# Row stage of a graph network's first hypergraph convolution: grouped moments, a later projection, four banks

## The chip, the cores and the metric

The kernel runs on one core of one Trainium2 chip. Its metric is the device time of one execution in microseconds (us): the median of several runs. Before the change it is 4742.29 us (median of 3 runs, 4738.69 to 4744.97).

Names used below: TensorE (PE in the profile; PEld is its weight load), VectorE (DVE), ScalarE (ACT), GpSimd (POOL) and SyncE (SP), which here issues transfers only. SBUF is the on-chip memory of 128 partitions, PSUM the eight banks that TensorE writes to.

## The reference

A graph of 3125 nodes with 256 features and 50,000 edges goes through four residual layers. Each begins with a layer norm (without weights) and a relu. The fourth layer, cut to what matters here:

```python
h = jnp.maximum(_layernorm(x, axis=-1), 0.0)
x = x + _L3_gnn_ref(h, edge_index, edge_weight, ...)

def _hconv(x, src, dst, ew, w1, b1, w2, b2, g, b):
    h = jax.nn.relu(x @ w1 + b1)                     # rows: the stage of this change (first call)
    msg = ew[:, None] * h[src]
    agg = jax.ops.segment_sum(msg, dst, num_segments=x.shape[0])
    h = agg @ w2 + b2
    return jax.nn.relu(_bn(h, g, b))                 # batch norm over all nodes

h = _hconv(x, ..., c1_w1, c1_b1, ...)
h = jax.nn.relu(_bn(h, bn1_g, bn1_b))
h = _hconv(h, ..., c2_w1, c2_b1, ...)
h = _bn(h, bn2_g, bn2_b)
return jax.nn.relu(h + residual)
```

All of it is float32. The layer norm takes, for each node, mean and variance over its 256 features.

## The kernel before

The 3125 nodes are padded to 25 tiles (`NT`) of 128 rows; `X` holds all of them in SBUF, one tile being 128 partitions by 256 columns. The program is a sequence of phases. The last is `tail()` (from line 1461). In it each engine has its own list of instructions in one block (lines 1664 to 1768), and semaphores order the engines against each other; within an engine the written order holds. There is no planner: the order is written out by hand.

`tail()` does this, one after the other:

1. An aggregation (`add_steps`, `multiply_steps`, `gather_pairs`, `ready_pairs`, signals `agr`) that ends the third layer and adds into `X`. GpSimd gathers rows by indirect DMA, VectorE builds one-hot matrices (line 212), TensorE multiplies into the four PSUM banks `ps` (line 301), VectorE adds (line 228).
2. **The stage of this change**: layer norm and relu of `X`, and `relu(h @ w1 + b1)`, whose rows go to `feat_d` in device memory. The functions are `dve_normalise` (line 1527), `act_normalise` (1544) and `pe_normalise` (1562), called at lines 1728, 1704 and 1752.
3. The first convolution's aggregation, the same four functions, which gathers from `feat_d`; GpSimd starts when all five `stored` semaphores have counted every store (lines 1696 to 1698).
4. Its transposes and matmuls with `w2` (`pe_convolve`, `act_convolve`), two batch norms, and the second convolution's projection (`pe_project(pe, 1, n, ...)`, line 1760, with `dve_bias` at 1736 and `act_rectify` at 1716 and 1719).
5. Aggregation, matmuls and batch norms of the second convolution, and the output.

In stage 2 a tile goes through these steps: VectorE takes its moments (`bn_stats`, 1530) and puts them together (`bn_aggr`, 1538); ScalarE takes the square root (1548); VectorE takes the reciprocal (1535) and the shift, minus mean times reciprocal (1540); ScalarE normalises and rectifies into `HB` (1552); TensorE turns it by two transposes into a bank `pt` (1568); ScalarE copies that to `ht` (1558); TensorE projects it with two float32 matmuls, four instructions in the profile, into a bank `pf` (1524); VectorE adds the bias into one of five `stage` buffers (1519); ScalarE rectifies it in place (1514); SyncE stores it (1510).

The loops interleave tiles. In step j VectorE issues moments of tile j, bias of tile j - 3, reciprocal of tile j - 1, aggregate of tile j and shift of tile j - 1, with two `drain`s, which hold the engine until its earlier results are written. ScalarE issues root j, normalise j - 1, copy j - 2, rectify j - 4. TensorE turns tile n and then projects tile n - 1. `pt`, `pf` and `ht` have two buffers each. A bias waits for the projection of its tile and for the store that last used its `stage` buffer, five tiles earlier.

Of the kernel before, what the change touches and what calls it, by code (L numbers as in the profile page):

```python
# [5 lines left out]
ALU = mybir.AluOpType  # L6
# [7 lines left out]
P = 128  # L14
N = 3125
E = 50000
D = 256
HEADS = 4
HD = D // HEADS
KD = D // P  # L20
# [40 lines left out]
def gnn_program(nc, t, out):  # L61
# [1399 lines left out]
    def tail():  # L1461
# [16 lines left out]
        ht = sb("t_ht", [P, 2, D])  # L1478
# [7 lines left out]
        pf = [psum(f"t_pf{k}", [P, 512]) for k in range(2)]  # L1486
        feat_rows = feat_d.rearrange("(n p) f -> n p f", p=P)
# [28 lines left out]
        def dve_bias(dve, z, n):  # L1516
            dve.wait_ge(s_proj, NT * z + n + 1)
            wait_from(dve, stored[n % 5], 16 * (5 * z + n // 5))
            dve.tensor_tensor(stage[:, n % 5, :], pf[n % 2][:, 0:D], b1[:, z, :], ALU.add).then_inc(s_bias, 1)

        def pe_project(pe, z, n, source):
            wait_from(pe, s_bias, NT * z + n - 1)
            for c in range(KD):
                last = pe.matmul(pf[n % 2][:, 0:D], source(c), W1[:, z, c, :], start=(c == 0), stop=(c == KD - 1))
            last.then_inc(s_proj, 1)

        def dve_normalise(dve):
            for j in range(NT + 3):
                if j < NT:
                    dve.bn_stats(stats[:, j, :], X[:, j, :])  # L1530
                if j >= 3:
                    dve_bias(dve, 0, j - 3)
                if 1 <= j <= NT:
                    dve.wait_ge(s_root, j)
                    dve.reciprocal(rstd[:, j - 1:j], rstd[:, j - 1:j])
                dve.drain()
                if j < NT:
                    dve.bn_aggr(mv[:, j, :], stats[:, j, :]).then_inc(s_var, 1)
                if 1 <= j <= NT:
                    dve.scalar_tensor_tensor(out=shift[:, j - 1:j], in0=mv[:, j - 1, 0:1], scalar=-1.0,  # L1540
                                             in1=rstd[:, j - 1:j], op0=ALU.mult, op1=ALU.mult).then_inc(s_shift, 1)
                dve.drain()

        def act_normalise(act):
            for j in range(NT + 4):
                if j < NT:
                    act.wait_ge(s_var, j + 1)
                    act.activation(rstd[:, j:j + 1], mv[:, j, 1:2], ACT.Sqrt, bias=eps[:, 0:1]).then_inc(s_root, 1)
                if 1 <= j <= NT:
                    n = j - 1  # L1550
                    act.wait_ge(s_shift, n + 1)
                    act.activation(HB[:, n, :], X[:, n, :], ACT.Relu, bias=shift[:, n:n + 1],
                                   scale=rstd[:, n:n + 1]).then_inc(s_norm, 1)
                if 2 <= j <= NT + 1:
                    n = j - 2
                    act.wait_ge(s_ht, n + 1)
                    wait_from(act, s_proj, n - 1)
                    act.copy(ht[:, n % 2, :], pt[n % 2][:, 0:D]).then_inc(s_htc, 1)
                if j >= 4:
                    act_rectify(act, 0, j - 4)  # L1560

        def pe_normalise(pe):
            for n in range(NT + 1):
                if n < NT:
                    pe.wait_ge(s_norm, n + 1)
                    wait_from(pe, s_htc, n - 1)
                    for c in range(KD):
                        last = pe.transpose(pt[n % 2][:, c * P:(c + 1) * P], HB[:, n, c * P:(c + 1) * P], ident[:, :])
                    last.then_inc(s_ht, 1)
                if n >= 1:  # L1570
                    pe.wait_ge(s_htc, n)
                    pe_project(pe, 0, n - 1, lambda c: ht[:, (n - 1) % 2, c * P:(c + 1) * P])
# [236 lines left out]
```

## Time and profile before

| what | value |
|---|---|
| median of 3 runs | 4742.29 us |
| the profiled execution's own time | 4777.76 us |
| its span | 4775.9 us |
| busy share of the span: PE, PEld, DVE, ACT, POOL | 50%, 36%, 44%, 30%, 50% |
| mean granted clock of TensorE (1 is 2.4 GHz) | 0.706 |
| HBM traffic | 97 GB/s over the span |

The span runs from the first to the last instruction of one profiled execution; busy is time in which an engine worked on an instruction. The shares are means over phases that differ much, so a single stage has to be read from its own stretch. The granted clock is what the chip's throttle gave TensorE, as a share of full speed: 0.50 is 1.2 GHz. Times in rows are microseconds from the span's start.

### The profile page before, as it was taken

How to read it: one execution, taken by the hardware profiler on the slowest of the kernel's cores; microseconds unless marked ns; L12 is line 12 of the kernel's file. 1: busy time of each engine (PE TensorE's matmuls, PEld its weight loads, DVE VectorE, ACT ScalarE, POOL GpSimd, SP SyncE). 2: the span in 40 equal slices, each digit the busy share in tenths (PEclk: the TensorE clock that was granted, in tenths of full speed). 3: DMA queues.
4: the chain of work that ended last, by engine and by line, in shares of the span. 5: the costliest groups of instructions: out<-in, count | busy, mean ns of one | idle time of the engine just before them, and what ended most of it. 6: DMA issues, size and time to landing. Idle time of an engine off the chain costs nothing. (4 is left out here: it accounts for less than half of the span.)

```text
span 4775.9 us, 63970 instructions
## 1 busy us (share of the span) xinstructions
PE 2383.8 (50%) x11271; PEld 1719.6 (36%) x11272; DVE 2090.5 (44%) x5486; ACT 1423.7 (30%) x4674; POOL 2384.7 (50%) x2446
## 2 busy tenths in 40 slices
PE   4301546665431255555665825556535557445556
PEld 2201534444320154444443313334324334223334
DVE  6502974444330189444447613334213334223336
ACT  2201746666530155566666600000200000200002
POOL 4774015555547500455553466663166663466660
PEclk9655977777665588677767957667556678667667
DMA  3443433333234344233324833331133331223331
GB/s 113 123 107 93 128 107 93 101 101 97 65 89 118 108 116 127 83 98 98 102 80 115 273 92 91 90 91 57 53 91 90 90 91 43 92 85 90 91 90 38
DMA packets 339579, 465.59 MB, mean 97 GB/s; under 512 B 108191, under 2 KB 253928, under 8 KB 336112
## 3 DMA queue, kind: packets, MB, share of 16 engines
q0 software_dynamic: 113824, 289.70, 21.1%
q1 hardware_dynamic: 157536, 109.12, 8.1%
q10 hardware_dynamic: 67956, 64.45, 4.7%
q14 instruction: 243, 1.99, 0.1%
q8 instruction: 20, 0.33, 0.0%
HBM read 385.88 MB, written 76.97 MB: 97 GB/s over the span
## 5 line engine op out<-in xcount | busy, mean ns | idle before, releaser
L301 PE MATMUL t_ps<-t_ring,t_hot 128*128 x2640 | 891.1, 503 | 905.0 <-DVE t_hot L212 467.8
L153 POOL DMA_INDIRECT ring<-feat_d,srcC x784 | 754.6, 962 | 1084.0 <-ACTq L167 842.5
L301 PEld LDWEIGHTS t_ps<-t_ring,t_hot 128*128 128x128 f32 x2640 | 644.7, 255 | 1152.2 <-issue 1036.4
L153 POOL DMA_INDIRECT t_ring<-feat_d,srcC x784 | 741.9, 946 | 563.7 <-issue 218.3
L175 ACT ACTIVATE ring<-ring,exC 128x64 f32<-128x64 f32 x3136 | 818.9, 338 | 113.4 <-issue 110.5
L301 PE MATMUL bank<-ring,arena 128*128 x1760 | 648.8, 505 | 109.6 <-ACT ring L175 52.8
L910 PE MATMUL wide<-arena 128*128 128x100 bf16 x4704 | 272.9, 216 | 462.5 <-issue 228.4
L509 POOL DMA_INDIRECT attr_d<-abuf,attr_pos x392 | 405.6, 1035 | 191.6 <-issue 129.2
L228 DVE TENSOR_TENSOR acc<-acc,t_ps 128x256 f32 x440 | 184.4, 419 | 715.0 <-DMA arena<-in_L_gnn_ar 212.4
L153 POOL DMA_INDIRECT t_ring<-rel_d,relC x392 | 371.2, 947 | 227.4 <-issue 115.1
L301 PEld LDWEIGHTS bank<-ring,arena 128*128 128x128 f32 x1760 | 406.1, 256 | 188.8 <-issue 133.7
L212 DVE TENSOR_SCALAR t_hot<-lane,dlocT,weightT 128x128 f32<-128x128 f32 x1320 | 409.1, 356 | 103.0 <-issue 71.1
L291 PE MATMUL wide<-arena 128*128 x880 | 244.1, 369 | 414.7 <-DVE arena L220 311.9
L910 PEld LDWEIGHTS wide<-arena 128*128 128x128 bf16 x4704 | 237.2, 102 | 498.6 <-issue 285.2
L291 PEld LDWEIGHTS wide<-arena 128*128 128x128 f32 x880 | 209.7, 257 | 521.7 <-issue 486.7
L1602 ACT COPY t_ring<-t_pt 128x256 f32<-128x256 f32 x26 | 9.6, 370 | 1204.0 <-PE t_pt L1593 1204.0
L877 DVE TENSOR_TENSOR arena<-wide,masks 128x800 f32<-128x800 f32 x196 | 191.0, 974 | 308.0 <-remote 306.7
L228 DVE TENSOR_TENSOR acc<-acc,bank 128x261 f32 x440 | 187.6, 426 | 229.3 <-issue 117.8
L228 DVE TENSOR_TENSOR X<-X,t_ps 128x256 f32 x220 | 92.0, 418 | 359.7 <-DMA X<-in_x 206.4
L206 DVE TENSOR_TENSOR arena<-lane,dlocT 128x256 f32<-128x256 f32 x440 | 185.2, 421 | 117.5 <-issue 103.1
L829 ACT ACTIVATE arena<-arena,ones 128x512 bf16<-128x512 bf16 x196 | 141.9, 724 | 289.6 <-remote 282.7
L220 DVE TENSOR_SCALAR arena<-lane,arena,minus_tile 128x128 f32<-128x128 f32 x440 | 159.1, 361 | 137.9 <-issue 81.2
(266 smaller groups left out, 2271.0 us busy)
## 6 DMA issues: line engine op xcount, KB each, us to landing
arena<-lo_d ACTq DMA_DIRECT2D x392, 128.0 KB
rel_d<-mid_stage SPq DMA_DIRECT2D x25, 1024.0 KB, 4.4
arena<-attr_d SPq DMA_DIRECT2D x98, 260.0 KB
abuf<-in_attr SPq DMA_DIRECT2D x56, 448.0 KB
ring<-feat_d,srcC POOLq DMA_INDIRECT x784
t_ring<-feat_d,srcC POOLq DMA_INDIRECT x784
feat_d<-arena ACTq DMA_DIRECT2D x50, 128.0 KB
feat_d<-t_stage SPq DMA_DIRECT2D x50, 128.0 KB, 1.7
```

Source lines behind the costliest of these rows:

```text
L153: pool.indirect_dma_start(out=ring[:, u % RING, j, 0:D], out_offset=None, in_=table, in_offset=bass.IndirectOffsetOnAxis(ap=index[:, u, j: ...
L175: last = act.activation(part_of_row, part_of_row, ACT.Copy, scale=exC[:, bass.ds(u, 1), j, h])
L206: last = dve.tensor_tensor(hot[:, k % NHOT, :, :], lane[:, :].unsqueeze(1).to_broadcast([P, 2, P]), dlocT[:, bass.ds(s, 1), :].rearrange(" ...
L212: last = dve.tensor_scalar(hot[:, k % NHOT, j, :], lane[:, :], dlocT[:, bass.ds(s, 1), j], weightT[:, bass.ds(s, 1), j], ALU.is_equal, ALU ...
L220: dve.tensor_scalar(hot_a[:, k % NHOT, :], lane[:, :], aring[:, slot, AW - 1:AW], minus_tile[:, g.attr, bass.ds(s, 1)], ALU.subtract, ALU. ...
L228: dve.tensor_tensor(acc[:, tile, 0:g.width], acc[:, tile, 0:g.width], ps[k % NHOT][:, 0:g.width], ALU.add).then_inc(g.added, 1)
L291: pe.matmul(ps_a[k % NHOT][:, 0:AW - 1], hot_a[:, k % NHOT, :], aring[:, slot, 0:AW - 1], start=True, stop=True).then_inc(g.attr_done, 1)
L301: last = pe.matmul(ps[k % NHOT][:, 0:g.width], hot[:, k % NHOT, j, :], ring[:, slot, j, 0:g.width], start=(j == 0), stop=(j == 1))
L509: pool.indirect_dma_start(out=attr_d, in_=abuf[:, g % 2, k, :], in_offset=None, out_offset=bass.IndirectOffsetOnAxis(ap=attr_pos[:, at + k ...
L829: act.activation(looked[:, k % 2, 1, :], apart[:, k % 2, :], ACT.Relu, scale=-1.0, bias=ones[:, 0:1]).then_inc(s_dst_hot[l], 1)
L877: dve.tensor_tensor(cand[:, k % 2, :, :, :], pk[k % 2][:, :, :].rearrange("p b (s x) -> p (b s) x", x=P)[:, :, 0:HEADS * NT] .rearrange("p ...
L910: last = pe.matmul(pk[k % 2][:, j // 2, at:at + HEADS * NT], looked[:, k % 2, q, j * P:(j + 1) * P], tab[:, piece, q * HEADS * NT:(q + 1) ...
```

## The change

Buffers: `ht` grows from two tiles to four. The turn uses four banks, `pt` and the aggregation's `ps[2:4]`; the projection uses four, `pf` and `ps[0:2]`. The waits for a bank or a buffer now look back four tiles and not two, in the second convolution's projection too.

VectorE: the 25 tiles are divided in four groups (0 to 1, 2 to 7, 8 to 15, 16 to 24). For each group it takes all moments, drains once, puts all of them together, signals once, waits for one square root over the whole group, and takes one reciprocal and one shift over the group. In the last group the biases of tiles 0 to 4 stand behind the moments of tiles 20 to 24; the other twenty biases follow behind the group.

ScalarE: one square root per group, in front of the steps j = 0, 1, 4 and 9. Step j then has normalise j, copy j - 1, rectify j - 5.

TensorE: turn n, then projection n - 2.

```diff
@@ -1475,7 +1475,7 @@
         b2 = sb("t_b2", [P, 2, KD])
         gb = sb("t_gb", [P, 2, 2, 2, KD])
         eps = sb("t_eps", [P, 2])
-        ht = sb("t_ht", [P, 2, D])
+        ht = sb("t_ht", [P, 4, D])
         stage = sb("t_stage", [P, 5, D])
         tmp = sb("t_tmp", [P, 3, D])
         bn = sb("t_bn", [P, KD, NR, 6])
@@ -1484,6 +1484,8 @@
         ps = [psum(f"t_ps{k}", [P, 512]) for k in range(NHOT)]
         pt = [psum(f"t_pt{k}", [P, 512]) for k in range(2)]
         pf = [psum(f"t_pf{k}", [P, 512]) for k in range(2)]
+        p_turn, p_proj = pt + ps[2:4], pf + ps[0:2]
+        LN_GROUPS = [(0, 2), (2, 8), (8, 16), (16, NT)]
         feat_rows = feat_d.rearrange("(n p) f -> n p f", p=P)
 
         g_rel = Steps("agr", life, False)
@@ -1516,60 +1518,71 @@
         def dve_bias(dve, z, n):
             dve.wait_ge(s_proj, NT * z + n + 1)
             wait_from(dve, stored[n % 5], 16 * (5 * z + n // 5))
-            dve.tensor_tensor(stage[:, n % 5, :], pf[n % 2][:, 0:D], b1[:, z, :], ALU.add).then_inc(s_bias, 1)
+            dve.tensor_tensor(stage[:, n % 5, :], p_proj[n % 4][:, 0:D], b1[:, z, :], ALU.add).then_inc(s_bias, 1)
 
         def pe_project(pe, z, n, source):
-            wait_from(pe, s_bias, NT * z + n - 1)
+            wait_from(pe, s_bias, NT * z + n - 3)
             for c in range(KD):
-                last = pe.matmul(pf[n % 2][:, 0:D], source(c), W1[:, z, c, :], start=(c == 0), stop=(c == KD - 1))
+                last = pe.matmul(p_proj[n % 4][:, 0:D], source(c), W1[:, z, c, :], start=(c == 0), stop=(c == KD - 1))
             last.then_inc(s_proj, 1)
 
+        def group_of(n):
+            return next(g for g, (a, b) in enumerate(LN_GROUPS) if a <= n < b)
+
         def dve_normalise(dve):
-            for j in range(NT + 3):
+            def roots(g):
+                a, b = LN_GROUPS[g]
+                dve.wait_ge(s_root, g + 1)
+                dve.reciprocal(rstd[:, a:b], rstd[:, a:b])
+                dve.drain()
+                dve.scalar_tensor_tensor(out=shift[:, a:b], in0=mv[:, a:b, 0], scalar=-1.0, in1=rstd[:, a:b],
+                                         op0=ALU.mult, op1=ALU.mult).then_inc(s_shift, 1)
+
+            biased = 0
+            for g, (a, b) in enumerate(LN_GROUPS):
+                for n in range(a, b):
+                    dve.bn_stats(stats[:, n, :], X[:, n, :])
+                    if g == len(LN_GROUPS) - 1 and n >= a + 4:
+                        dve_bias(dve, 0, biased)
+                        biased += 1
+                dve.drain()
+                for n in range(a, b):
+                    last = dve.bn_aggr(mv[:, n, :], stats[:, n, :])
+                last.then_inc(s_var, 1)
+                roots(g)
+            for n in range(biased, NT):
+                dve_bias(dve, 0, n)
+
+        def act_normalise(act):
+            for j in range(NT + 5):
+                for g, (a, b) in enumerate(LN_GROUPS):
+                    if j == (0, 1, 4, 9)[g]:
+                        act.wait_ge(s_var, g + 1)
+                        act.activation(rstd[:, a:b], mv[:, a:b, 1], ACT.Sqrt, bias=eps[:, 0:1]).then_inc(s_root, 1)
                 if j < NT:
-                    dve.bn_stats(stats[:, j, :], X[:, j, :])
-                if j >= 3:
-                    dve_bias(dve, 0, j - 3)
-                if 1 <= j <= NT:
-                    dve.wait_ge(s_root, j)
-                    dve.reciprocal(rstd[:, j - 1:j], rstd[:, j - 1:j])
-                dve.drain()
-                if j < NT:
-                    dve.bn_aggr(mv[:, j, :], stats[:, j, :]).then_inc(s_var, 1)
-                if 1 <= j <= NT:
-                    dve.scalar_tensor_tensor(out=shift[:, j - 1:j], in0=mv[:, j - 1, 0:1], scalar=-1.0,
-                                             in1=rstd[:, j - 1:j], op0=ALU.mult, op1=ALU.mult).then_inc(s_shift, 1)
-                dve.drain()
-
-        def act_normalise(act):
-            for j in range(NT + 4):
-                if j < NT:
-                    act.wait_ge(s_var, j + 1)
-                    act.activation(rstd[:, j:j + 1], mv[:, j, 1:2], ACT.Sqrt, bias=eps[:, 0:1]).then_inc(s_root, 1)
+                    act.wait_ge(s_shift, group_of(j) + 1)
+                    act.activation(HB[:, j, :], X[:, j, :], ACT.Relu, bias=shift[:, j:j + 1],
+                                   scale=rstd[:, j:j + 1]).then_inc(s_norm, 1)
                 if 1 <= j <= NT:
                     n = j - 1
-                    act.wait_ge(s_shift, n + 1)
-                    act.activation(HB[:, n, :], X[:, n, :], ACT.Relu, bias=shift[:, n:n + 1],
-                                   scale=rstd[:, n:n + 1]).then_inc(s_norm, 1)
-                if 2 <= j <= NT + 1:
-                    n = j - 2
                     act.wait_ge(s_ht, n + 1)
-                    wait_from(act, s_proj, n - 1)
-                    act.copy(ht[:, n % 2, :], pt[n % 2][:, 0:D]).then_inc(s_htc, 1)
-                if j >= 4:
-                    act_rectify(act, 0, j - 4)
+                    wait_from(act, s_proj, n - 3)
+                    act.copy(ht[:, n % 4, :], p_turn[n % 4][:, 0:D]).then_inc(s_htc, 1)
+                if j >= 5:
+                    act_rectify(act, 0, j - 5)
 
         def pe_normalise(pe):
-            for n in range(NT + 1):
+            for n in range(NT + 2):
                 if n < NT:
                     pe.wait_ge(s_norm, n + 1)
-                    wait_from(pe, s_htc, n - 1)
+                    wait_from(pe, s_htc, n - 3)
                     for c in range(KD):
-                        last = pe.transpose(pt[n % 2][:, c * P:(c + 1) * P], HB[:, n, c * P:(c + 1) * P], ident[:, :])
+                        last = pe.transpose(p_turn[n % 4][:, c * P:(c + 1) * P], HB[:, n, c * P:(c + 1) * P],
+                                            ident[:, :])
                     last.then_inc(s_ht, 1)
-                if n >= 1:
-                    pe.wait_ge(s_htc, n)
-                    pe_project(pe, 0, n - 1, lambda c: ht[:, (n - 1) % 2, c * P:(c + 1) * P])
+                if n >= 2:
+                    pe.wait_ge(s_htc, n - 1)
+                    pe_project(pe, 0, n - 2, lambda c: ht[:, (n - 2) % 4, c * P:(c + 1) * P])
 
         def pe_convolve(pe, z):
             def chunk(r):
```

## Rows read from the trace of the kernel before

**Rows 1.** Timeline at the start of the stage: start us, us, engine, line, operation.

```profile
3326.75 0.43 DVE L1530 BATCH_NORM_STATS2 stats<-X 128x6 f32<-128x256 f32 x1
3327.25 0.18 DVE L1538 BATCH_NORM_AGGREGATE mv<-stats 128x2 f32<-128x6 f32 x1
3327.52 1.28 ACT L1548 ACT_TABLE_LOAD   x1 [600.76 <-DVE mv L1538]
```

**Rows 2.** Timeline at the end of the stage and the first gather behind it.

```profile
3424.90 3.62 PE L1524 MATMUL t_pf<-t_w,t_ht 128*128 128x256 f32 x8
...
3429.02 0.42 ACT L1514 ACTIVATE t_stage<-t_stage 128x256 f32<-128x256 f32 x1 [1.29 <-DVE t_stage L1519]
...
3431.90 0.97 POOL L153 DMA_INDIRECT t_ring<-feat_d,srcC  x1 [132.90 <-DMA feat_d<-t_stage]
```

**Rows 3.** Windows: length, busy of PE, PEld, DVE, ACT, POOL, granted clock, DMA.

```profile
3334.00:3380.00 46.00, 26.39 (x67) 16.50 (x67) 13.42 (x60) 15.58 (x46) 0.00 (x0) 0.50 0.08 29
```

**Rows 4.** Waits around the stage: who waits for whom, total us, times, longest.

```profile
DVE t_stage L1519 <- PE t_pf L1524: 68.1, 25, 3.3
```

**Rows 5.** Timeline, one period in the stage's middle, and the next period's first operation.

```profile
3358.04 0.42 DVE L1519 TENSOR_TENSOR t_stage<-t_pf,t_b 128x256 f32<-128x256 f32 x1 [2.75 <-PE t_pf L1524]
3358.38 0.15 DVE L1535 RECIPROCAL rstd<-rstd 128x1 f32<-128x1 f32 x1
3358.61 0.18 DVE L1538 BATCH_NORM_AGGREGATE mv<-stats 128x2 f32<-128x6 f32 x1
3358.70 0.13 DVE L1540 SCALAR_TENSOR_TENSOR shift<-mv,rstd 128x1 f32<-128x1 f32 x1
3358.82 0.30 ACT L1548 ACTIVATE rstd<-mv,t_eps 128x1 f32<-128x1 f32 x1 [2.69 <-DVE mv L1538]
...
3359.03 0.59 ACT L1552 ACTIVATE HB<-X,shift,rstd 128x256 f32<-128x256 f32 x1
3359.52 0.35 ACT L1558 COPY t_ht<-t_pt 128x256 f32<-128x256 f32 x1
...
3359.67 0.69 PE L1568 MATMUL t_pt<-ident,HB 128*128 128x128 f32 x2 [1.66 <-ACT HB L1552]
3359.77 0.42 ACT L1514 ACTIVATE t_stage<-t_stage 128x256 f32<-128x256 f32 x1
...
3362.10 0.42 DVE L1519 TENSOR_TENSOR t_stage<-t_pf,t_b 128x256 f32<-128x256 f32 x1 [2.75 <-PE t_pf L1524]
```

**Rows 6.** The projection's banks: one projection matmul, duration ns min/median/max.

```profile
L1524 PE MATMUL t_pf<-t_w,t_ht x100: 631/634/656, 3331.7 to 3427.9; 128*128 128x256 f32 x100
```

**Rows 7.** Line 1568, the turn's transposes, duration ns min/median/max.

```profile
L1568 PE MATMUL t_pt<-ident,HB x50: 273/421/477, 3330.5 to 3424.7; 128*128 128x128 f32 x50
```

**Rows 8.** Timeline, start of the second convolution's projection.

```profile
4077.34 14.83 PE L1524 MATMUL t_pf<-t_w,t_ring 128*128 128x256 f32 x56 [15.63 <-ACT t_ring L1624]
...
4081.16 0.42 DVE L1519 TENSOR_TENSOR t_stage<-t_pf,t_b 128x256 f32<-128x256 f32 x1 [1.28 <-PE t_pf L1524]
...
4082.71 0.42 DVE L1519 TENSOR_TENSOR t_stage<-t_pf,t_b 128x256 f32<-128x256 f32 x1 [1.13 <-PE t_pf L1524]
...
4083.58 0.42 DVE L1519 TENSOR_TENSOR t_stage<-t_pf,t_b 128x256 f32<-128x256 f32 x1 [0.44 <-PE t_pf L1524]
```

**Rows 9.** Timeline, first turns behind each convolution's aggregation.

```profile
4026.77 0.66 PE L1593 MATMUL t_pt<-ident,acc 128*128 128x128 f32 x4 [0.65 <-DVE acc L228]
4027.25 0.37 ACT L1602 COPY t_ring<-t_pt 128x256 f32<-128x256 f32 x1 [597.82 <-PE t_pt L1593]
...
4701.39 0.37 ACT L1602 COPY t_ring<-t_pt 128x256 f32<-128x256 f32 x1 [598.81 <-PE t_pt L1593]
```

**Rows 10.** Windows: the first convolution's matmuls and the second projection.

```profile
4020.00:4077.00 57.00, 36.33 (x135) 20.17 (x133) 30.17 (x72) 24.40 (x45) 5.44 (x1) 0.90 0.00 1
4077.00:4103.00 26.00, 24.33 (x100) 20.24 (x100) 10.61 (x25) 17.70 (x38) 0.00 (x0) 0.90 0.35 121
```

**Rows 11.** Line 1510, the stores of finished rows: issue to landing.

```profile
DMA to landing us min/median/max: 1.7/1.7/1.8
```

## The prediction

> **What bounds the kernel now.** I first looked at which stretch the change touches, then at who waits for whom in it, then at one period of its loop. The stretch is the one in which the first convolution's rows are made: from the first moments (`bn_stats`, 3326.75) to the last rectification (3429.02 + 0.42 = 3429.44), 102.7 us [rows 1, 2]. I count t from 3326.75, so it ends at t = 102.7. In its middle no engine is full: of 46 us TensorE is busy 26.4, VectorE 13.4, ScalarE 15.6, at a granted clock of 0.50, which is 1.2 GHz [rows 3]. VectorE alone waits 68.1 us in 25 waits for the projection [rows 4]. One period shows why [rows 5]: bias (3358.04), reciprocal, aggregate (3358.61), square root (3358.82, after 2.69 us of waiting for that aggregate), normalise (3359.03), copy (3359.52), and the next bias at 3362.10, after 2.75 us of waiting for the projection that follows the copy. That is 4.06 us, all of it a ring through three engines: VectorE puts the next tile's aggregate behind the bias, the bias waits for the projection, and the projection waits for a copy that ScalarE issues behind a square root that needs that aggregate. 25 tiles cost 25 x 4.06 = 101.5 us: the ring is the stage.
>
> When the stage ends, GpSimd's first gather starts 2.46 us later, at 3431.90 [rows 2]. It waits for the last store, so every microsecond taken from the stage moves all that follows.
>
> **The change, part by part.**
>
> *The ring is cut.* No bias stands ahead of a moment that an earlier tile still needs, except five in the last group. What is left per tile are three independent rates. ScalarE: normalise to copy 0.49, copy to rectify 0.25, rectify 0.42 [rows 5] less the same overlap of 0.10, so 0.32: 1.06 us. Twenty-one of 25 square roots go (0.30 us each, off the path by then). VectorE: one operation of 256 columns per 0.34 us (bias 3358.04, reciprocal 3358.38 [rows 5]); bias and moments together 0.68, later the bias alone. TensorE at 1.2 GHz: eight projection matmuls take 3.62 us with 0.634 for one [rows 2, 6], so (3.62 - 0.63) / 7 = 0.427 each, 1.71 us a tile; its two turns take 0.69 us [rows 5] with 0.42 to 0.48 for one [rows 7], 0.21 to 0.27 apart, taken as 0.25 each: together 2.21 us. At 2.4 GHz: the same four matmuls, in the second convolution's projection, come every 0.87 us (biases at 4082.71 and 4083.58) [rows 8], and turns stand 0.13 apart ((0.66 - 0.27) / 3) [rows 7, 9]; with 0.27 for two, 1.14 us a tile. So TensorE is the next bound at either clock, just ahead of ScalarE at the upper one.
>
> *Which clock.* In the second projection TensorE comes out of 15.6 us without work, and its biases at 4081.16 and 4082.71 stand 1.55 us apart; from 4082.71 they stand 0.87 apart. So some 5.4 us of unbroken matmuls (4077.34 to 4082.7) stood before the full rate, and it held to the end at 0.90 mean [rows 8, 10]. In the convolution, with TensorE busy 36.3 of 57 us, the clock is 0.90 too [rows 10]. After the change TensorE has a queue of work from t = 7, and at the low clock it needs more time than it gets tiles, so it doesn't pause until the clock has risen. I take the rise at t = 12.3.
>
> *The head, step by step* (starts in t; hand-over between engines 0.03 to 0.11, estimated from [rows 1, 5]). Group of tiles 0 and 1: moments 0.00 and 0.34, aggregates 0.84 and 0.94 (0.50 from the last moment to the first aggregate [rows 1], 0.10 from one small operation to the next [rows 5]), table load of 1.28 at 1.21, root 2.49, reciprocal 2.82, shift 3.06, normalise 0 at 3.22. Group of 6: from 3.16, 6 x 0.34 + 0.16 + 6 x 0.10, last aggregate ends 6.04; ScalarE is held in front of tile 1 for it; root 6.07, normalise 1 at 6.27, turn 1 at 6.97. Group of 8: VectorE takes 6.74 to 10.5; root 10.53; shift 11.10. Group of 9: five moments to 12.9, then four moments and five biases in turn. The biases need projections 0 to 4. TensorE: turns 1, 2, projection 0 (1.71), turn 3, projection 1 to about 12.0 at the low clock, then 1.14 a tile, so projection 4 ends near 16.0. Bias 4 at 16.2, drain, nine aggregates to 17.6; root; normalise 9 at 17.9. ScalarE's rectifications 0 to 3, which stand ahead of that root in its queue, are done by 17.0. TensorE has by then eight turns and seven projections behind it: 8 x 0.27 + 7 x 0.87 = 8.2 us at the upper clock, and 2.6 more for 5.3 us at the lower, out of 11.6: it hardly idles.
>
> *The rest.* Turn 9 at 18.6; then 16 x 0.27 = 4.3 for turns and 18 projections x 0.865 = 15.6 bring TensorE to 38.5. The last matmul's length over its spacing 0.2 (0.634 less 0.427), bias 0.42, rectify 0.42, hand-overs 0.06: the stage ends at t = 39.6 in place of 102.7. That is 63.1 us less. The last store and the first gather keep their 2.46 us.
>
> *What I cost at nothing.* Four banks in place of two: the two added pairs are the aggregation's, which has ended before and has not begun after; VectorE's last bias stands ahead of the first add in its queue. Stores: a tile's 128 KB land in 1.7 us [rows 11], a stage buffer is wanted again five tiles, so 5 x 1.14 = 5.7 us, later; between a turn's end and its bias five tiles on lie 4.3 us, against about 2.6 for copy, rectification, issue and landing. If that cover went (landing above 3.4 us) each tile would pay a fifth of the excess. The second convolution's projection keeps its matmul rate: VectorE waits for TensorE at its biases [rows 8], so two more banks bring 0. The clock handed to the aggregation behind: it costs nothing, because ScalarE's idle time over the first convolution's aggregation, entered at a low clock, is 597.8 us and over the second's, entered at 0.90, 598.8 [rows 9].
>
> *A rule weighed.* The rows show turns 0.13 us apart, 0.66 us for four, right behind an aggregation [rows 9]. The Trainium skill (TensorE: Matmul & The Clock Gate, Part 4: PE-mode transpose) says that the full clock doesn't engage for transposes. The trace disagrees with it where turns are mixed with matmuls; by the rule the turns would stay 0.25 apart, and the sum would be 50 x 0.12 = 6 us less gain.
>
> **Bounds of the sum.** Best: the clock is high throughout and the head costs TensorE nothing, 7.0 + 24 x 0.27 + 25 x 0.87 + 1.1 = 36.3, a gain of 66. Worst for the clock is the first rival.
>
> **Rivals.**
> 1. *The clock stays at 1.2 GHz.* The head's pauses, or the turns among the matmuls, keep it low, as in this stage before [rows 3]. TensorE from t = 7.0: 24 x 0.50 + 25 x 1.71 = 54.8, plus 1.1: end at 62.9, gain 39.8, 4702.5 us. For it: it is what this stage showed. Against: TensorE would then be at work without a break, and [rows 8] shows the rise in that case.
> 2. *A shorter ring binds.* If ScalarE's copy of a tile has to come before the normalise of the next, each tile costs turn 0.27, copy 0.25 + 0.1, rectify 0.32, normalise 0.59, hand-over 0.11: 1.65 us. I count it as going round once per two tiles, as ScalarE's order has normalise one tile ahead of copy; if once per tile, 16 x (1.65 - 1.14) = 8 us are lost: 4687 us.
> 3. *Slower: the stores.* Bias n waits for store n - 5, and rectification now stands a step later. The stage would be longer than before if five tiles took over 20.3 us, so if a store landed later than about 18 us after issue. At a spacing of 0.87 us they land in 1.7 [rows 8, 11]; at 19 us each the stage would be 25 x 4.3 = 108 us, 4747 us. Only a transfer slowed tenfold does it.
> 4. *It doesn't do what it says:* another wait keeps the 4.06 us period, 4742 us. The order of the instructions leaves no ring that closes within one tile, and the 4.06 us rest on one.
>
> **How the numbers follow.** The profiled execution took 4777.76 us with a span of 4775.9; the median of the runs is 4742.29, 0.7% below. The stage holds no gathers, and I subtract its gain whole from the median: 4742.3 - 63.1 = 4679.2 (the profiled one would be 4714.7). Small hand-overs are more often left out than counted twice, so I say 4680. Chances: the forecast (4674 to 4685) 0.70; rival 2, or a head some microseconds longer (to 4692), 0.13; rival 1, or a clock that changes back and forth (4690 to 4706), 0.13; rival 3 0.02; rival 4 0.02. The range takes in rival 1's price: 4674 to 4703. What a measurement of this kernel can tell from no change is about 0.2%, 9.5 us; all of the first three cases lie beyond it: faster 0.96, same 0.02, slower 0.02.
>
> **What would show it.** The stretch from the first moments to the last rectification is about 40 us long. The four square roots stand near t = 2.5, 6.1, 10.5 and 17.6, and normalise 9 just behind the last. Between t = 20 and 38 biases are 1.14 us apart, TensorE is busy without a gap at a clock near 1, projection matmuls last 0.38 and not 0.63 us. VectorE's wait for projections is below 20 us. Biases 2.2 us apart with matmuls of 0.63 are rival 1; biases 1.6 apart with gaps on TensorE in front of turns rival 2; VectorE waiting for stores rival 3. The aggregation behind should keep its 598 us; if it is 5 us or more off, the prediction misses a coupling.

## The result

The changed kernel takes 4673.6 us (median of 4 runs, 4656.7 to 4681.82), the kernel before, in its runs of then and now, 4743.63 us: ratio 0.9852, 95% interval 0.9829 to 0.9875. By the medians that is 70.0 us less, where 63 were forecast; the interval reaches from 4662.5 to 4684.3 us (0.9829 and 0.9875 of 4743.63). The profiled execution took 4672.72 us (span 4671.0).

The first group is the timeline of the stage's head in the changed kernel (start us, us, engine, line, operation). It answers to [rows 1].

```profile
3298.32 0.75 DVE L1544 BATCH_NORM_STATS2 stats<-X 128x6 f32<-128x256 f32 x2
3299.15 0.25 DVE L1550 BATCH_NORM_AGGREGATE mv<-stats 128x2 f32<-128x6 f32 x2
3299.48 1.28 ACT L1561 ACT_TABLE_LOAD   x1 [594.63 <-DVE mv L1550]
3300.78 0.29 ACT L1561 ACTIVATE rstd<-mv,t_eps 128x2 f32<-128x2 f32 x1
...
3301.54 0.60 ACT L1564 ACTIVATE HB<-X,shift,rstd 128x256 f32<-128x256 f32 x1 [0.47 <-DVE shift L1538]
...
3303.55 0.51 DVE L1550 BATCH_NORM_AGGREGATE mv<-stats 128x2 f32<-128x6 f32 x6
3304.09 0.30 ACT L1561 ACTIVATE rstd<-mv,t_eps 128x6 f32<-128x6 f32 x1 [1.95 <-DVE mv L1550]
...
3304.94 0.69 PE L1580 MATMUL t_pt<-ident,HB 128*128 128x128 f32 x2 [2.24 <-ACT HB L1564]
...
3308.23 0.30 ACT L1561 ACTIVATE rstd<-mv,t_eps 128x8 f32<-128x8 f32 x1 [1.44 <-DVE mv L1550]
...
3314.57 0.30 ACT L1561 ACTIVATE rstd<-mv,t_eps 128x9 f32<-128x9 f32 x1
3314.78 0.58 ACT L1564 ACTIVATE HB<-X,shift,rstd 128x256 f32<-128x256 f32 x1
```

The second is the timeline of one period in the middle, then the last rectification and the first gather; it answers to [rows 2, 5].

```profile
3323.27 0.61 ACT L1564 ACTIVATE HB<-X,shift,rstd 128x256 f32<-128x256 f32 x1
3323.28 1.03 PE L1526 MATMUL t_ps<-t_w,t_ht 128*128 128x256 f32 x4
3323.76 0.37 ACT L1570 COPY t_ht<-t_pt 128x256 f32<-128x256 f32 x1
...
3324.01 0.44 ACT L1516 ACTIVATE t_stage<-t_stage 128x256 f32<-128x256 f32 x1
3324.14 0.38 PE L1580 MATMUL t_pt<-ident,HB 128*128 128x128 f32 x2
...
3324.34 0.42 DVE L1521 TENSOR_TENSOR t_stage<-t_ps,t_b 128x256 f32<-128x256 f32 x1 [0.66 <-PE t_ps L1526]
3324.36 1.03 PE L1526 MATMUL t_ps<-t_w,t_ht 128*128 128x256 f32 x4
...
3335.54 0.42 ACT L1516 ACTIVATE t_stage<-t_stage 128x256 f32<-128x256 f32 x1 [0.79 <-DVE t_stage L1521]
...
3338.42 0.94 POOL L153 DMA_INDIRECT t_ring<-feat_d,srcC  x1 [67.60 <-DMA feat_d<-t_stage]
```

The stage runs from 3298.32 to 3335.54 + 0.42 = 3335.96, 37.64 us, against 102.7: 65.1 us less. The first gather follows 2.46 us behind it, as before. The ring is gone: a tile takes TensorE 1.08 us (3323.28 and 3324.36), and it goes from projection to turn to projection (3323.28, 3324.14, 3324.36). ScalarE's 1.06 us a tile (3323.27, 3323.76, 3324.01, and the next normalise at 3324.33, which isn't shown) is just below it. In the head one sees the four roots (t = 2.5, 5.8, 9.9 and 16.3 from 3298.32) and normalise 9 right behind the last, at t = 16.46.

The windows of the changed kernel (length, busy time and count of PE, PEld, DVE, ACT, POOL, granted clock, DMA share, GB/s; they answer to [rows 3]) show the clock's way through the stage:

```profile
3298.30:3304.30 6.00, 0.41 (x2) 0.20 (x2) 3.81 (x18) 2.39 (x5) 0.00 (x0) 0.87 0.00 0
3304.30:3309.80 5.50, 4.79 (x15) 3.60 (x16) 4.79 (x23) 4.03 (x11) 0.00 (x0) 0.52 0.00 0
3309.80:3315.40 5.60, 5.60 (x31) 4.32 (x29) 5.03 (x24) 4.76 (x14) 0.00 (x0) 1.00 0.22 75
3315.40:3334.00 18.60, 18.60 (x103) 15.94 (x103) 7.56 (x19) 17.91 (x51) 0.00 (x0) 1.00 0.35 120
```

The clock is 1.00 until 3302.7, so still at turn 0 (3302.29), then 0.50 until 3309.5, from turn 1 (3304.94) on, and 1.00 again from 3309.6 (t = 11.2). TensorE is busy without a gap for the last 18.6 us shown. VectorE's waits for projections, 68.1 us before [rows 4], are 11.1 us (total, times, longest):

```profile
DVE t_stage L1521 <- PE t_ps L1526: 5.8, 9, 0.7
DVE t_stage L1521 <- PE t_pf L1526: 5.3, 8, 0.7
```

### The profile page after: what moved, and what is told of

Its sections match the earlier page's. It is cut to its first block and busy times, and to the rows that moved or that the text cites. A ratio compares the mean times of both kernels' runs of the same rounds, so it can differ in the third digit from the quotient of the medians.

```text
span 4671.0 us, 63853 instructions
## 1 busy us (share of the span) xinstructions
PE 2342.8 (50%) x11271; PEld 1694.6 (36%) x11272; DVE 2088.9 (45%) x5444; ACT 1410.8 (30%) x4653; POOL 2384.8 (51%) x2446
## 5 line engine op out<-in xcount | busy, mean ns | idle before, releaser
L234 DVE TENSOR_TENSOR acc_a<-acc_a,wide 128x129 f32 x440 | 127.5, 290 | 200.2 <-issue 129.2
```

What stands on the lines that cost most here:

```text
L234: dve.tensor_tensor(acc_a[:, tile, :], acc_a[:, tile, :], ps_a[k % NHOT][:, 0:AW - 1], ALU.add).then_inc(g.attr_added, 1)
```

## The experiments

Each stage length is that of one profiled execution. Each experiment was read twice: by the length of the stage in its trace, from the first moments to the last rectification (two executions of the changed kernel further down gave 37.85 and 37.68 us, so this repeats to 0.2 us), and by the time of the whole kernel, where the runs of one kernel lie 6 to 25 us apart. All ratios are to the kernel before on the same chip.

| kernel | stage us | time us | before us | ratio, 95% interval |
|---|---|---|---|---|
| before | 102.7 | 4743.63 | | |
| changed | 37.64 | 4673.6 | 4743.63 | 0.9852, 0.9829 to 0.9875 |
| e1, groups alone | 40.01 | 4710.28 | 4771.91 | 0.9867, 0.9836 to 0.9898 |
| e2, depth alone | 99.94 | 4765.03 | 4771.91 | 0.998, 0.9966 to 0.9995 |
| e3, depth and a late bias | 39.86 | 4707.81 | 4771.91 | 0.9858, 0.9832 to 0.9883 |
| e4, the change again | 37.85 | 4704.31 | 4771.91 | 0.9851, 0.9829 to 0.9873 |
| e7, bias five behind | 43.04 | 4704.38, one run | 4774.29 | |
| e8, before, TensorE kept busy | 80.07 | 4750.75 | 4774.29 | 0.9945, 0.9926 to 0.9965 |
| e6, change, busy start | 37.29 | 4718.8, one run | 4774.29 | |
| e5, shorter head | 38.62 | 4714.93 | 4774.29 | 0.9873, 0.9853 to 0.9892 |
| e9, head mended | 37.22 | 3529.39, one run | 3598.05 | |
| e10, the same and a busy start | 38.38 | 3534.89 | 3598.05 | 0.9829, 0.9816 to 0.9843 |
| e11, the change, third time | 37.68 | 3534.2 | 3598.05 | 0.9819, 0.9805 to 0.9833 |
| e12, rectification later | 36.66 | 3532.5 | 3598.15 | 0.9821, 0.9808 to 0.9835 |

### Which part of the change does it: e1, e2, e3, e7

e1 keeps the groups and takes back the depth:

```diff
-        p_turn, p_proj = pt + ps[2:4], pf + ps[0:2]
+        p_turn, p_proj = pt, pf
...
-                if n >= 2:
-                    pe.wait_ge(s_htc, n - 1)
-                    pe_project(pe, 0, n - 2, ...)
+                if n >= 1:
+                    pe.wait_ge(s_htc, n)
+                    pe_project(pe, 0, n - 1, ...)
```

> Grouped moments, grouped roots and late biases as in the change; but two banks and two turn buffers, and the projection one tile behind the turn, as before. Theory (the gain is that no bias stands any more in front of a moment, aggregate or shift in VectorE's queue): the stage from the first moments to the last rectification takes 38 to 42 us, against 102.7 before and 37.6 with the change, since only the head waits more for its banks; the time is within 0.2% of the changed kernel's. Rival (depth: banks and the later projection carry the gain): the stage takes over 60 us.

40.01 us: of the 65.1 us the groups alone bring 62.7. TensorE then stands once 1.55 and once 0.83 us in front of a projection until a bias has freed its bank, together 2.4 us, as much as the depth brings on top. (Not among the lines above: `ht` and the waits for banks go back to two as well.)

e2 keeps the depth and takes back the groups; VectorE and ScalarE go tile by tile as before, one step later (these lines against the kernel before):

```diff
-            for j in range(NT + 3):
+            for j in range(NT + 4):
                 if j < NT:
                     dve.bn_stats(stats[:, j, :], X[:, j, :])
-                if j >= 3:
-                    dve_bias(dve, 0, j - 3)
+                if j >= 4:
+                    dve_bias(dve, 0, j - 4)
```

> Four banks, four turn buffers and the projection two tiles behind the turn, as in the change; but moments, roots and shifts tile by tile as before, with each bias again in front of the next reciprocal and shift (bias of tile j - 4 in step j, one later than before as the projection is one later). Theory (order on VectorE): the ring through three engines is still closed within one tile, 3.3 to 4.1 us a tile at the low clock, the stage 85 to 103 us and the time within 0.4% of the kernel before. Rival (depth carries the gain): under 60 us for the stage, about 4680 us or below.

99.94 us: depth alone brings 2.8 us. Its timeline has the old period (the next bias stands 4.06 us on, at 3365.61), the bias with its wait for TensorE again in front of aggregate and shift:

```profile
3361.55 0.42 DVE L1521 TENSOR_TENSOR t_stage<-t_ps,t_b 128x256 f32<-128x256 f32 x1 [2.74 <-PE t_ps L1526]
...
3362.12 0.18 DVE L1543 BATCH_NORM_AGGREGATE mv<-stats 128x2 f32<-128x6 f32 x1
...
3362.54 0.58 ACT L1557 ACTIVATE HB<-X,shift,rstd 128x256 f32<-128x256 f32 x1
...
3363.18 0.69 PE L1573 MATMUL t_ps<-ident,HB 128*128 128x128 f32 x2 [1.66 <-ACT HB L1557]
...
3363.66 1.91 PE L1526 MATMUL t_pf<-t_w,t_ht 128*128 128x256 f32 x4
```

It also corrects one member of the ring. The prediction lets the projection wait for ScalarE's copy. In e2 that copy was made a tile earlier, and yet the projection starts 0.48 us behind the turn (3363.18, 3363.66), as it does in the kernel before (3359.67 in [rows 5], and this row):

```profile
3360.15 1.92 PE L1524 MATMUL t_pf<-t_w,t_ht 128*128 128x256 f32 x4
```

So what closes the ring on TensorE is its own order: bias, aggregate, root, normalise, then the turn of that tile, and the projection that stands behind this turn. That is why projecting a tile later and having more banks brought next to nothing.

e3 differs from e2 in one number on VectorE: the bias of tile j - 6 stands in step j, not that of j - 4 (rectification follows, at j - 7).

> As the run with depth alone (four banks, projection two behind, moments tile by tile, nothing grouped), with one edit: the bias of tile j - 6 stands in step j instead of j - 4. Theory: grouping is not needed, what counts is that the ring closes over three tiles; the pace is then set by ScalarE's 1.27 us or VectorE's 1.25 us a tile, 1.3 to 1.5 us, so the stage takes 42 to 50 us and most of the gain is there (4678 to 4690 us). Rival (the grouped moments carry it by saving drains, roots and hand-overs): over 70 us for the stage.

39.86 us, 60.1 less than e2, with nothing grouped. The theory holds; the stage came out 2 us below its range, as the pace was 1.21 to 1.25 us a tile. (The whole kernel's 4707.81 us lies above the 4678 to 4690 expected, because the kernel before takes 4771.91 us on this chip; the gain is 64.1 us.) The timeline shows why: the same operations in the same order (bias, aggregate), but the bias has nothing to wait for. What holds the pace instead stands in the window below it: ScalarE is busy 10.00 of 10.00 us.

```profile
3340.63 0.41 DVE L1521 TENSOR_TENSOR t_stage<-t_pf,t_b 128x256 f32<-128x256 f32 x1
...
3341.18 0.18 DVE L1543 BATCH_NORM_AGGREGATE mv<-stats 128x2 f32<-128x6 f32 x1
...
3341.84 0.41 DVE L1521 TENSOR_TENSOR t_stage<-t_ps,t_b 128x256 f32<-128x256 f32 x1
```

```profile
3340.00:3350.00 10.00, 10.00 (x50) 6.80 (x50) 8.59 (x43) 10.00 (x34) 0.00 (x0) 1.00 0.29 102
```

e7 puts the bias at j - 5 (rectification at j - 6).

> As the run with the late bias, but bias of tile j - 5 in step j, so that the ring closes over two tiles and not one or three. Theory (pace is the ring's length over the tiles that it spans, until an engine is full): a ring of 4.1 us at the low clock gives 2.05 us a tile, under TensorE's own 2.2, so TensorE is full, its clock rises, the ring shortens to about 3 us and the pace falls to 1.25 to 1.5 us: a stage of 40 to 47 us. Rival (anything in front of the shift in VectorE's queue costs its whole wait): over 60 us.

43.04 us, inside the range, at 1.48 us a tile with the clock at 1.00 (25 us from 3325). The two biases shown are two tiles apart, 2.96 us, which is the ring; in each a bias waits 0.28 us for TensorE, and no engine is full (TensorE 21.75, ScalarE 22.60 of 25 us):

```profile
3335.47 0.42 DVE L1521 TENSOR_TENSOR t_stage<-t_pf,t_b 128x256 f32<-128x256 f32 x1 [0.28 <-PE t_pf L1526]
...
3338.43 0.42 DVE L1521 TENSOR_TENSOR t_stage<-t_ps,t_b 128x256 f32<-128x256 f32 x1 [0.28 <-PE t_ps L1526]
```

One tile more between a bias and what it waits for is worth 56.9 us (from e2), the second 3.2 us. In these three runs the pace is the ring's length over the tiles that it spans, until an engine is full, and grouping is one of two ways out of the ring. They don't end at the same bound: the change is held by TensorE at 1.08 us a tile, e3, with a root per tile, by ScalarE at 1.25. That the stages still lie only 2.2 us apart is because e3's head has no groups to wait for (argued, not tested). Of e3's time some 1.3 us is a wait for a store at the end (2.3 us long, the last projection being done 2.57 us before the end of the stage and not 1.25 as in the change).

### How much of it is the clock: e8, e6

```diff
                     pe_project(pe, 0, n - 1, ...)
+                    for k in range(2):
+                        pe.matmul(ps[0][:, 0:D], ident[:, :], W1[:, 0, 0, :], start=True, stop=True)
```

> The kernel before, with two more float32 matmuls of 256 columns behind each projection, whose product nobody reads (they stand in TensorE's idle 1.66 us of each period). It tells how much of the 65 us is the low clock alone. Theory (the clock is an effect of the ring and lengthens it): the granted clock rises to near 1, projection 1.92 to 1.03 us and turns 0.69 to 0.4, so the period falls from 4.06 to about 3.05 us and the stage from 102.7 to 75 to 82 us, 20 to 28 us faster than before, although TensorE does more. Rival (the clock doesn't rise, or the ring isn't TensorE's): the stage stays at 100 us or grows to 105.

The stage falls to 80.07 us, 22.7 us less, by giving TensorE more to do; ratio 0.9945 (0.9926 to 0.9965). Its timeline and window:

```profile
3365.96 1.03 PE L1574 MATMUL t_ps<-t_w,ident 128*128 128x256 f32 x4
3366.16 0.42 DVE L1519 TENSOR_TENSOR t_stage<-t_pf,t_b 128x256 f32<-128x256 f32 x1 [1.74 <-PE t_pf L1524]
...
3367.15 0.58 ACT L1552 ACTIVATE HB<-X,shift,rstd 128x256 f32<-128x256 f32 x1
...
3368.06 1.11 PE L1524 MATMUL t_pf<-t_w,t_ht 128*128 128x256 f32 x4
...
3369.21 0.42 DVE L1519 TENSOR_TENSOR t_stage<-t_pf,t_b 128x256 f32<-128x256 f32 x1 [1.73 <-PE t_pf L1524]
```

```profile
3335.00:3400.00 65.00, 49.05 (x214) 35.69 (x213) 24.41 (x106) 28.21 (x83) 0.00 (x0) 0.98 0.12 41
```

The period is 3.05 us, the projection takes 1.1 us and not 1.92, the granted clock is 0.98. The two added matmuls (3365.96 to 3366.99) are done before the tile behind them is normalised, so they hold nothing up. So of the 65.1 us that the change brings, 22.7 can be had by the clock alone with the ring left as it is, and 42.4 need the ring to be cut. The low clock was an effect of the ring and made it a third longer; the prediction took both together, through the rate at the upper clock.

e6 is the changed kernel with ten such matmuls before its first turn.

> The changed kernel with ten float32 matmuls of 256 columns, read by nobody, before TensorE's first turn, so that it comes into the head at the high clock. Theory (in the head VectorE and ScalarE set the pace, TensorE has slack): the stage takes 37.3 to 37.8 us, the same as with the change, and TensorE shows longer gaps before turns of tiles 1 to 9. Rival (the cold head costs what it takes more, 2.6 us): about 35 us.

37.29 us, at the lower edge of the range, 0.35 below the change. That is less of a test than it was meant to be: behind a pause of 2.30 us in front of turn 1 the clock fell again, from 3337.5 to 3340.8 (t = 10.0). So the low stretch was halved, 3.3 us in place of 6.8, and the stage became 0.35 us shorter; a head that is at the high clock throughout is seen only in e10, with another order.

### Is there more than the stage: e4, e11

> The changed kernel itself, to tell whether its 70 us of gain, against 65.05 us in the stage's own stretch, are real beyond the stage. Theory: the rest is scatter of the gather phases, which the change doesn't touch: over these runs the median gain comes to 60 to 70 us, the stage again takes 37.5 to 37.8 us, and the three aggregations of the last phase move by several us from one execution to the next in no relation to the change. Rival (the denser stage also speeds the aggregation behind it): the first convolution's aggregation is shorter than the second's by 3 us or more, and the gain is 68 to 75 us.

> The changed kernel itself, on the chip of the two runs above. The stage takes 37.6 to 37.9 us. Its gain over the kernel before is 63 to 70 us if the stage is all there is; over 70 us again would speak for an effect beyond it, in the aggregations behind.

By the medians the gains are 67.6 us (e4) and 63.9 us (e11). ScalarE stands idle through each aggregation behind the stage, so its idle time at the first copy gives the length. Two rows of the changed kernel's timeline, answering to [rows 9]:

```profile
3930.49 0.37 ACT L1615 COPY t_ring<-t_pt 128x256 f32<-128x256 f32 x1 [594.53 <-PE t_pt L1606]
...
4596.44 0.37 ACT L1615 COPY t_ring<-t_pt 128x256 f32<-128x256 f32 x1 [590.77 <-PE t_pt L1606]
```

The first convolution's took 597.8 us before and 594.5 here, the second's 598.8 and 590.8; and the aggregation in front of the stage, which the change can't touch, 600.8 [rows 1] and 594.6 (3299.48 in the head above). All three were shorter in this one execution (3.3, 8.0 and 6.2 us), the one in front no less than the others. The rival wants the first to be at least 3 us shorter than the second. In e4 it is 596.1 against 597.9, in e11 500.8 against 499.5, in the profiled execution of the change 3.8 us longer, and before the change it was 1.0 shorter. The gains of e4 and e11 are short of the rival's 68 us too. A second reading says the same: from the stage's end to the kernel's end the execution of the change took 1335.0 us, but e4 1343.3, e1 1343.7, e3 1344.1, e5 1345.1, e7 1345.6 and e6 1349.0 with a short stage, and e2 and e8, with a long one, 1343.8 and 1343.7. So the rival is refuted, and what lies between 65 and 70 us is scatter of phases that the change leaves alone. (These are executions of their own: the profiled one of the kernel before took 4777.76 us, more than any of the four runs in its median.)

### A version meant to be better: e5, e9, e10, e12

e5 loads ScalarE's square root table ahead of the phase, takes the second and the third root one step later and makes two more biases early.

```diff
+                act.wait_ge(s_eps, 1)
+                act.activation(bsc[:, 0, 0:1], eps[:, 0:1], ACT.Sqrt, bias=eps[:, 0:1])
                 ready_pairs(act, "agr", g_rel, ring)
...
-                    if j == (0, 1, 4, 9)[g]:
+                    if j == (0, 2, 5, 9)[g]:
...
-                    if g == len(LN_GROUPS) - 1 and n >= a + 4:
+                    if g == len(LN_GROUPS) - 1 and n >= a + 2:
```

> A version meant to be better: the changed kernel with ScalarE's square root table loaded at the start of the phase (one root of a constant, read by nobody), the second group's root behind normalise 1 and not in front of it (steps 0, 2, 5, 9), and seven early biases, two moments earlier. Theory (the head of 16 us is a chain of table load, moments and roots): the table load's 1.28 us goes and TensorE starts tile 1 about 2 us earlier; the stage takes 34.5 to 36.2 us, which the time of the whole kernel (scatter 20 us) can hardly show. Rival (TensorE's or ScalarE's total is what counts from the first tile): 36.3 us or more, only the table load's share.

38.62 us, 1 us worse than the change. The early biases run at TensorE's pace, and the last group's aggregates stand behind them; ScalarE waits 2.52 us for those and TensorE 2.14 for ScalarE. It is the old fault once more, inside the head: a bias that waits, in front of aggregates.

```profile
3345.82 0.42 DVE L1521 TENSOR_TENSOR t_stage<-t_pf,t_b 128x256 f32<-128x256 f32 x1 [0.33 <-PE t_pf L1526]
...
3346.91 0.42 DVE L1521 TENSOR_TENSOR t_stage<-t_ps,t_b 128x256 f32<-128x256 f32 x1 [0.33 <-PE t_ps L1526]
3347.43 0.71 DVE L1550 BATCH_NORM_AGGREGATE mv<-stats 128x2 f32<-128x6 f32 x9
3348.17 0.30 ACT L1561 ACTIVATE rstd<-mv,t_eps 128x9 f32<-128x9 f32 x1 [2.52 <-DVE mv L1550]
...
3349.01 0.44 PE L1580 MATMUL t_pt<-ident,HB 128*128 128x128 f32 x2 [2.14 <-ACT HB L1564]
```

e9 takes that away: three early biases (`n >= a + 6`) and roots at steps (0, 2, 5, 8).

> The shorter head again, with what held it taken away: seven early biases had put two that wait for projections in front of the last group's aggregates. Now the table load is ahead of the phase, the roots stand at steps 0, 2, 5 and 8, and only three biases (tiles 0 to 2) stand in front of the last aggregates. Theory (a waiting bias in front of the aggregates costs its wait, in the head as in the old ring): TensorE's 2.1 to 2.5 us gap before tile 9 goes and the stage takes 35.6 to 36.6 us, against 38.62 in the run with seven and 37.7 to 37.9 with the change. Rival (the fewer early biases hold TensorE for its banks): 37.5 us or more.

37.22 us, below the rival's 37.5 but not in the theory's 35.6 to 36.6. The gap before tile 9 is gone and one before tile 6 has come: bias 0 is now late, ScalarE's rectification 0 waits for it, and normalise 6 is queued behind the rectification.

```profile
2350.11 0.41 DVE L1521 TENSOR_TENSOR t_stage<-t_pf,t_b 128x256 f32<-128x256 f32 x1
...
2350.55 0.42 ACT L1516 ACTIVATE t_stage<-t_stage 128x256 f32<-128x256 f32 x1 [1.97 <-DVE t_stage L1521]
...
2350.87 0.58 ACT L1564 ACTIVATE HB<-X,shift,rstd 128x256 f32<-128x256 f32 x1
...
2351.51 0.44 PE L1580 MATMUL t_ps<-ident,HB 128*128 128x128 f32 x2 [1.39 <-ACT HB L1564]
```

e10 is e9 with the ten matmuls of e6.

> The mended head with ten matmuls of 256 columns, read by nobody, in front of TensorE's first turn. Alone they brought 0.4 to 0.5 us. Theory (with the shorter head TensorE is what everything waits for sooner, so its low clock costs more): the stage takes 34.4 to 35.8 us, 2 to 3 us less than the change. Over the whole kernel that is 0.06%, which its time won't show: the ratio to the kernel before should be that of the change within its interval. Rival: TensorE's pause between tiles 1 and 2 lets the clock fall again, and the stage takes what it takes without the added matmuls (35.6 us or more).

38.38 us, worse than e9: the theory fails. The rival's lower bound (35.6 us) is met, and the clock did fall, but not behind the pause that the rival names (between tiles 1 and 2, 1.54 us). The head runs at a clock of 1.00, so TensorE comes to the gap before tile 6 earlier and stands 2.24 us; after it the clock falls, and 3.2 us (2353.0 to 2356.2) run at the low rate. Its windows, and two rows of its timeline:

```profile
2345.00:2351.00 6.00, 4.77 (x24) 3.57 (x24) 5.48 (x25) 3.05 (x9) 0.00 (x0) 1.00 0.01 1
2351.00:2357.00 6.00, 4.76 (x17) 3.90 (x18) 3.74 (x19) 4.91 (x14) 0.00 (x0) 0.72 0.25 87
2357.00:2375.00 18.00, 18.00 (x100) 15.49 (x99) 7.02 (x17) 17.51 (x49) 0.00 (x0) 1.00 0.34 117
```

```profile
2352.24 0.44 PE L1580 MATMUL t_ps<-ident,HB 128*128 128x128 f32 x2 [2.24 <-ACT HB L1564]
...
2354.23 1.92 PE L1526 MATMUL t_pf<-t_w,t_ht 128*128 128x256 f32 x4
```

e12 is e9 with rectification one step later in ScalarE's queue (tile j - 6 in step j).

> The mended head with one more edit: rectification of tile j - 6 in ScalarE's step j instead of j - 5. In the mended head ScalarE waited 1.97 us in front of rectification 0 for bias 0, with normalise 6 queued behind it, and TensorE then stood 1.39 us in front of tile 6. Theory (the same rule as for the ring, a waiting operation costs what is queued behind it): normalise 6 no longer stands behind that wait, TensorE's gap before tile 6 shrinks to under 0.5 us, and the stage takes 35.3 to 36.3 us against 37.22. Rival (TensorE then waits for its banks instead, as projection 4 needs bias 0): 36.8 us or more. The time of the whole kernel stays within the interval of the changed one's.

36.66 us, the shortest stage of all, 1.0 us below the changed kernel in e11 (on another chip, where the kernel before takes the same time), 0.4 us above the range of the theory and below the rival's. TensorE has no gap from its third turn on (2347.94, t = 5.9) to its last projection. That is worth 0.6 of the 1.0 us; the other 0.4 stand at the very end, where the last bias waits 0.2 us for a store and not 0.85 as in e11. What is left of the head is the low clock, which lasted until t = 12.0. Over the whole kernel, 3532.5 us against 3534.2 tells nothing; the better version is shown in its stage alone.

## Why the prediction was wrong where it was

- **The step that failed: "I subtract its gain whole from the median".** That puts at nothing, without a reason, what a median of whole runs carries from the phases outside the stage. With the stage as measured it would have given 4742.3 - 65.1 = 4677.2, inside the range; 4.9 of the 70.0 us that the medians show lie outside the stage. The runs show scatter there: the changed kernel's four lie 25.1 us apart, those of before 6.3 (15.8 with the fourth), and the same code in front of the stage took from 3324.2 to 3339.7 us in the four runs of one chip (e1 to e4). The lower end, 4674, lies 2.3 us below the prediction's own best case (4742.3 - 66 = 4676.3), while the prediction puts at 9.5 us what a measurement can tell apart. The median came out 0.4 us below that end; forecast and sum (4680 and 4679.2) lie within the measured interval, 4662.5 to 4684.3. On which side of 4674 the median fell was luck. What sets the time of the untouched phases from run to run stays open.
- **The sum, a smaller step: 63.1 forecast, 65.1 measured in the stage.** It stayed within the best case, 66. The mis-sized term is the head: 17.9 us forecast for normalise 9, 16.46 measured. Of these 1.4 us, 1.2 stand already at bias 4 (16.2 forecast, 14.99 measured), which waits for projection 4. From projection 1's end, about 12.0, three tiles of 1.14 us give 15.4 and not the 16.0 written down; and TensorE was at that point by 11.6, as the clock had risen at t = 11.2 and not 12.3. The rest is the small operations: an aggregate takes (0.51 - 0.15) / 5 = 0.07 us and not 0.10. Behind the head TensorE took 1.08 us a tile and not 1.14, which the store at the end (below) in part takes back. "Small hand-overs are more often left out than counted twice" led to 4680 from 4679.2, and was the wrong way.
- **The ring and its cut: right, but for one member.** The bias in front of the next aggregate closes it: e2 has the ring with all the depth, e3 is free of it with nothing grouped. The projection was held by the turn in front of it, not by the copy (e2).
- **TensorE as the next bound, clock near 1: right.** 1.08 us a tile against 1.14 forecast; ScalarE 1.06 as worked out.
- **Rival 1 (low clock):** did not come; e8 gives its measure, 22.7 us of the old stage. **Rival 2 (a shorter ring):** there is none in the steady part. In the head waits of this kind exist, as e5 and e9 show. **Rival 3 (stores):** nearer than the prediction thought, which costed them at nothing. A store lands in 1.7 us as a rule, but in up to 3.1 in the changed kernel and 3.5 in e3 (1.8 at most before [rows 11]). In the change one bias (24) waits 0.78 us for a store, of which 0.34 delay the end; in e3 it is 2.3 us. **Rival 4:** no.
- **The Trainium skill's rule on transposes** (TensorE: Matmul & The Clock Gate, Part 4: PE-mode transpose): the turns lie 0.11 us apart at a granted clock of 1.00 ((1.08 - 0.87) / 2), so the trace stays against it for turns mixed with matmuls. A long stretch of turns alone is in no run here.

## What to carry to other kernels

In a loop over several engines whose instructions run in the written order, find the operation that waits for the slowest hand-over and look at what is queued behind it that an earlier stage of the next tile needs: moving that one operation back by one or two tiles can be worth more than all banks and buffers. Look also at which instruction the slow hand-over really waits behind: an engine's own order can hold it where the program's wait doesn't. Don't read the granted clock as a given: here the ring left TensorE idle for part of each period, the clock stood at 0.50 and made the ring a third longer, and work that nobody reads raised it to 0.98. When the range of a forecast is worked out from one stage, add the scatter of the medians: here the interval was 22 us wide, and the stage was missed by 2.

## What the runs showed of the hardware

- On the two chips of e9 to e12 the kernel before takes 3598.05 and 3598.15 us and not 4771.91, with the same program. The aggregations of this phase take some 500 us there and not 597 (ScalarE's idle time over the last one: 499.5 in e11, 597.9 in e4); the stage takes 37.68 us as elsewhere, and the change's gain in microseconds is nearly the same (63.9 and 67.6), so its ratio differs. Why the gathers are faster there was not examined.
- The clock can fall behind a pause of TensorE of 2.2 us: behind that of 2.24 us in e10 the granted clock of the 6 us window is 0.72 and a projection takes 1.92 us again; behind one of 2.30 us in e6, between the turns of tiles 0 and 1, the first projection took 1.91. The pause before tile 9 in e5 was 2.14 us, and the projections behind it took 1.03 us. In the changed kernel itself the clock was still 1.00 behind a pause of 4.66 us, at turn 0 (3302.29), and 0.50 from 3302.8 on. So the length of the pause just before doesn't tell alone; what decides the runs don't show.
- ScalarE's operations grow longer in the steady part of the changed kernel, normalise from 0.58 us (3314.78) over 0.61 (3323.27) to 0.64 (3330.69), with no change in shape or place. It cost nothing here and stays unexplained.
